# Mamba mixer stage: the residual moved from VectorE to ScalarE and GpSimd, and the next tile's squares moved into the loop over heads

## The reference, cut to what matters

```
residual = hidden_states
h = rmsnorm(hidden_states, norm_w)
z, xBC, dt = split(h @ in_proj.T)
xBC = silu(conv(xBC) + conv_b)          # causal convolution of width 4 over the tokens
dt = softplus(dt + dt_bias);  A = -exp(A_log)
y = scan over tokens: state = state * exp(dt*A) + dt*B*x;  y = state*C;  y += D*x
y = rmsnorm(y * silu(z), ssm_norm_w)
h = residual + y @ out_proj.T
```

## Time and profile before

| quantity | value |
|---|---|
| median of three runs | 2724.34 us (2722.08 to 2725.27) |
| the profiled execution | 2722.0 us, of which the span of instructions 2720.2 us |
| mixer, from the start to L912 of tile 7 | 830 us |
| one tile in the steady part (L912 to L912) | 101.11 to 101.13 us |
| granted TensorE clock, mean | 0.999 |

### The profile page before, as it was taken

The page is one execution under the profiler, slowest core; times in us unless marked ns, Lnnn a source line. Parts: engine busy times, 40 slices in busy tenths (PEclk is TensorE's granted clock), DMA queues, the critical chain, the costliest instruction groups (busy, mean ns, idle before and its releaser), DMA issues.

```text
span 2720.2 us, 42348 instructions
## 1 busy us (share of the span) xinstructions
PE 2659.7 (98%) x15264; PEld 2070.4 (76%) x15264; DVE 1523.4 (56%) x2561; ACT 1019.5 (37%) x2375; POOL 693.8 (26%) x594
## 2 busy tenths in 40 slices
PE   7999999999999999999999989999999999999999
PEld 5777777777778888888888867777777777777776
DVE  8787797797795322332233277777777774111122
ACT  6334334334434222122212255555555553222221
POOL 6553553553561101000100101322233322000000
PEclk9999999999999999999999999999999999999999
DMA  4001001101114101110111211110111124211111
GB/s 154 27 21 47 31 15 46 44 3 46 46 48 140 62 1 62 62 62 0 62 62 48 73 70 48 63 40 29 62 54 62 58 64 150 82 47 46 46 46 47
DMA packets 85482, 147.83 MB, mean 54 GB/s; under 512 B 4032, under 2 KB 17984, under 8 KB 85408
## 3 DMA queue, kind: packets, MB, share of 16 engines
q1 hardware_dynamic: 85408, 146.84, 15.7%
HBM read 113.27 MB, written 33.55 MB: 54 GB/s over the span
## 4 chain that ended last, share of the span: by engine, by line
PE 88%; DVE 8%; issue 2%; ACT 1%; DMA 1%; DVEq 0%; SPq 0%; POOL 0%; ACTq 0%; POOLq 0%
PE ps L75 22%; PE ps L77 22%; PE ps L76 22%; PE ps L1770 4%; PE ps L2133 4%; PE ps L816 2%; PE ps L1782 2%; PE ps L1761 2%; DVE mx_m L608 1%; DVE mx_cv L600 1%; PE ps L792 1%; PE ps L804 1%; PE ps L747 1%; PE ps L1714 1%; PE ps L844 1%
## 5 line engine op out<-in xcount | busy, mean ns | idle before, releaser
L1471 ACT ACTIVATE at_pr<-ps,at_nm 128x256 f32<-128x256 f32 x512 | 235.6, 473 | 201.7 <-DVE at_nm L1621 201.7
L1162 DVE TENSOR_TENSOR gm_m_lo<-gm_m,gm_m_hi 128x512 fp32r<-128x512 f32 (+1 forms) x88 | 61.1, 694 | 416.9 <-ACT gm_m_hi L1079 416.9
L75 PE MATMUL ps<-sh_u_hi,gm_gu_hi 128*128 128x512 f32 (+1 forms) x704 | 274.9, 390 | 0.0
L76 PE MATMUL ps<-sh_u_lo,gm_gu_hi 128*128 128x512 f32 (+1 forms) x704 | 274.8, 390 | 0.0
L77 PE MATMUL ps<-sh_u_hi,gm_gu_lo 128*128 128x512 f32 (+1 forms) x704 | 274.7, 390 | 0.0
L1627 DVE COPY at_pT<-ps 128x512 f32<-128x512 f32 x256 | 176.3, 689 | 138.5 <-PE ps L1770 136.4
L1073 ACT ACTIVATE gm_sg<-ps 128x512 f32<-128x512 f32 (+1 forms) x88 | 52.7, 599 | 517.6 <-PE ps L77 517.4
L543 POOL TENSOR_TENSOR mx_m<-mx_m,mx_g 128x512 f32<-128x512 f32 x128 | 185.4, 1448 | 86.3 <-DVE mx_m L610 86.1
L75 PE MATMUL ps<-sh_u_hi,qm_w_hi 128*128 128x512 f32 x512 | 201.6, 394 | 2.1 <-issue 1.1
L77 PE MATMUL ps<-sh_u_hi,qm_w_lo 128*128 128x512 f32 x512 | 199.6, 390 | 0.0
L76 PE MATMUL ps<-sh_u_lo,qm_w_hi 128*128 128x512 f32 x512 | 199.4, 389 | 0.0
(11 more groups left out here) (252 smaller groups left out, 6352.6 us busy)
## 6 DMA issues: line engine op xcount, KB each, us to landing
sh_xf<-x_scratch SPq DMA_DIRECT2D x16, 1024.0 KB, 7.5
mx_xr<-in_x SPq DMA_DIRECT2D x8, 1024.0 KB, 5.6
h_scratch<-mx_xr SPq DMA_DIRECT2D x8, 1024.0 KB, 5.1
sh_xf<-h_scratch SPq DMA_DIRECT2D x8, 1024.0 KB, 8.4
gm_xr<-in_x SPq DMA_DIRECT2D x8, 1024.0 KB, 7.3
gm_r<-h_scratch SPq DMA_DIRECT2D x8, 1024.0 KB, 6.1
x_scratch<-gm_r SPq DMA_DIRECT2D x8, 1024.0 KB, 5.2
at_cf<-in_ctxT SPq DMA_DIRECT2D x16, 512.0 KB, 3.9
```

Source lines behind the costliest of these rows:

```text
L75: nc.tensor.matmul(out, l_hi, r_hi, start=first, stop=False)
L76: nc.tensor.matmul(out, l_hi, r_lo, start=False, stop=False)
L1471: A(pr[h][:, t, :], SC[h][:, SEQ * t:SEQ * t + SEQ], ACT.Exp, bias=nm[:, 4 * n + h, t:t + 1], accum_out=sums[:, 2 * b + t, 4 * g + h:4 * g ...
```

## The change

- The residual of tiles 0 to 6 is no longer made by DVE. ACT copies a PSUM bank, scaled by `rg`, into m0 (`scale_out`), and GpSimd adds m0 to `xr`. The order of banks is 2, 3, 0, 1. The first two copies stand at the end of ACT's tile, the other two between its first and second tap of the next tile. Tile 7 keeps the old way.
- PE's wait before `conv_in(2)` for the whole residual becomes four waits, of `conv_in(2)` to `conv_in(5)`, each for the copy of its own bank. DVE's first scan of a tile waits for GpSimd's adds.
- The four squares of the next tile move from the convolution into the loop over heads, j = 0 to 3. The four norms move from j = 1 to 4 to j = 5 (two) and j = 6 (two).
- GpSimd makes the reciprocal roots for these norms after head 9 instead of before head 0.

```diff
+    OUT = (2, 3, 0, 1)
 # ACT
+        def scale_out(i, n):
+            t = OUT[n]
+            act.wait_ge(s["out"], KI * i + KI)
+            act.wait_ge(s["y"], KI * i + KI)
+            act.wait_ge(s["rg"], i + 1)
+            A(m0[t][:, :], ps[t][:, :], ACT.Copy, scale=rg[:, t:t + 1]).then_inc(s["ho"], 1)
...
             if step_0(i):
                 exp_ln(i)
+            else:
+                scale_out(i - 1, 2)
+                scale_out(i - 1, 3)
             tap(i, 1)
...
-                if n >= 5:
-                    square(i + 1, n - 5)
...
-                if 1 <= j <= TT:
-                    norm(i + 1, j - 1)
+                if j < TT:
+                    square(i + 1, j)
+                elif j in (5, 6):
+                    norm(i + 1, 2 * j - 10)
+                    norm(i + 1, 2 * j - 9)
...
                 exp_ln(i + 1)
+                scale_out(i, 0)
+                scale_out(i, 1)
 # POOL
-            first(i + 1)
...
+                if h == 9:
+                    first(i + 1)
             add_squares(i, 7)
-            at(pool, s["h1"], TT * i)
+            at(pool, s["ho"], TT * i)
...
+            for n, t in () if final(i) else enumerate(OUT):
+                pool.wait_ge(s["ho"], TT * i + n + 1)
+                G(xr[:, t, :], xr[:, t, :], m0[t][:, :], ALU.add).then_inc(s["h1"], 1)
 # DVE
+            if h == 0:
+                at(dve, s["h1"], TT * i)
...
-            for t in range(TT):
+            for t in range(TT) if final(i) else ():
                 V.scalar_tensor_tensor(xr[:, t, :], ps[t][:, :], rg[:, t:t + 1], xr[:, t, :], ALU.mult,
 # PE
+            if 2 <= n <= 5:
+                at(pe, s["ho"], TT * (i - 1) + n - 1)
             if n >= 4:
                 pe.wait_ge(s["cv"], 3 * NCONV * i + 3 * (n - 3))
-            elif n == 2:
-                at(pe, s["h1"], TT * i)
```

More of the change, by code:

```diff
@@ L345, in stage_mixer @@
     names = ("x0 xr st dtp dtc dtt in G dat bc zp xt y out ss a nab ee u ln c rec c2 sp dt dta da dah dal "
-             "dac tap cv sl Ge z xd sc M t g gs glo acc sse rg h1").split()
+             "dac tap cv sl Ge z xd sc M t g gs glo acc sse rg ho h1").split()
     s = {**sh.s, **{k: sem(f"mx_{k}") for k in names}}
     me.s = s
+    OUT = (2, 3, 0, 1)
     def ahead(i):
@@ L546, in main @@
                     add_squares(i, (h - 3) // 2)
+                if h == 9:
+                    first(i + 1)
             add_squares(i, 7)
-            at(pool, s["h1"], TT * i)
+            at(pool, s["ho"], TT * i)
             pool.wait_ge(s["sse"], i + 1)
             G(rg[:, :], v0[:, :], mhalf[:, :], ALU.pow).then_inc(s["rg"], 1)
+            if not final(i):
+                pool.wait_ge(s["xr"], 16 * i + 16)
+            for n, t in () if final(i) else enumerate(OUT):
+                pool.wait_ge(s["ho"], TT * i + n + 1)
+                G(xr[:, t, :], xr[:, t, :], m0[t][:, :], ALU.add).then_inc(s["h1"], 1)
         pool.wait_ge(su.dve, dve_0 + 4)
@@ L723, in main @@
                 dt_second(i + 1)
-            dve.wait_ge(s["out"], KI * i + KI)
-            dve.wait_ge(s["xr"], 16 * i + 16)
-            dve.wait_ge(s["rg"], i + 1)
-            for t in range(TT):
+            if final(i):
+                dve.wait_ge(s["out"], KI * i + KI)
+                dve.wait_ge(s["xr"], 16 * i + 16)
+                dve.wait_ge(s["rg"], i + 1)
+            for t in range(TT) if final(i) else ():
                 V.scalar_tensor_tensor(xr[:, t, :], ps[t][:, :], rg[:, t:t + 1], xr[:, t, :], ALU.mult,
```

## The result

| | before | after |
|---|---|---|
| median of six runs | 2724.35 us (2721.6 to 2725.27) | 2737.28 us (2736.12 to 2739.71) |
| ratio, 95% interval | | 1.005 [1.0037, 1.0063] |
| span of the profiled execution | 2720.2 us | 2734.8 us |
| one looped tile | 101.1 us | 103.0 us |

What follows compares the result with a forecast made beforehand. PE was taken to bound the kernel, with one 1.9 us hole a tile. 7 x 1.75 + 1.3 = 13.5 us slower gave 2735.5 against the profiled execution, 2737.8 as median; range 2731 to 2745, chance 0.80.

Steps and rivals of the forecast that it cites:

- The term that counts: Late norms behind ACT's square at j = 6 delay PE's next-tile transposes: 1.75 us in tiles 0 to 6, 1.3 in tile 7.
- The terms set at nothing: Moved residual, squares and root: each forecast to cost 0 and gain 0.
- The residual on ACT and GpSimd: Start of a tile: ACT's copies at 0.78 us and GpSimd's adds at 1.29 us fit without delaying PE; cost 0.
- The squares: Leaving the convolution shortens nothing, as ACT waited 1.11 us for PE before the tap; 0 on both sides.
- The root after head 9: GpSimd's two small instructions take about 1.3 us, head 11 keeps over 3 us of room before PE wants it; cost 0.
- the hole: PE's 1.9 us of waits per tile, for GpSimd's multiplied decays and ACT's silu; forecast to stay.
- (1): Rival: DVE's saved 2.73 us a tile close PE's 1.9 us hole, sum +0.2, 2724.5 us; chance 0.06.
- (2): Rival: the transposes' wait is hidden, PE coming later or the norms earlier, 2724.3 us; chance 0.05.
- (3): Rival: GpSimd's adds hold up DVE's small steps in `dt_third`, say 1 us a tile, +7, 2744.8 us; chance 0.04.
- (4): Rival: PE's new pause drops the granted clock, 1.45 us in each of seven tiles, 10.2, 2748.0 us; chance 0.03.

Runs made afterwards that it cites:

- experiment 1: Changed kernel with norms 0 and 1 at j = 4, norms 2 and 3 at j = 5: 2724.39 us, ratio 1.0004.
- experiment 2: Kernel before with only the norms moved, two at j = 5 and two at j = 6: 2738.15 us, ratio 1.0052.
- experiment 4: Changed kernel with three norms at j = 5 and one at j = 6: 2734.11 us, ratio 1.0036.
- experiment 3: Kernel before with only the residual moved to ACT and GpSimd; squares, norms and root as before: 2725.42 us, ratio 1.0006.
- experiment 6: Kernel of experiment 1 with the two first scans of a tile moved into the convolution: 2724.56 us, ratio 1.0005.
- experiment 7: Kernel before with the two first scans of a tile moved into the convolution: 2723.43 us, ratio 1.0001.
- experiment 8: Experiment 6 plus, in tiles 1 to 7, first x transposes, head 2's spread and scan ahead of the last convolution channel: 2714.5 us, ratio 0.9958.
- experiment 9: Experiment 7 plus, in tiles 1 to 7, first x transposes, head 2's spread and scan ahead of the last convolution channel: 2713.02 us, ratio 0.9954.
- experiment 5: Kernel of experiment 1 with DVE's wait for GpSimd's adds moved from before the first scan to before convolution channel 8: one execution, 2727.35 us.

## Why the prediction was right

**The term that counts.** The step was: the norm ends at 417.68, the transpose starts 1.75 us later than before, 7 times, and 1.3 more in tile 7. Measured: 1.72 a tile in tiles 1 to 6, from the same pieces (0.52, 1.32, 0.13 against 0.52, 1.33, 0.15), and tile 7 longer by 1.28 (100.05 against 98.77 from sum to sum), with the 0.35 that PE waited there before gone, as forecast. Experiments 1 and 2 show that this placement is necessary and sufficient for the loss, experiment 4 that the wait follows the length of ACT's queue.

**The terms set at nothing.** The residual on ACT and GpSimd: shown by experiment 3, and no wait of PE names them. The copies took 0.68 to 0.69 each, under the 0.78 taken. The squares: ACT's idle time in the convolution grew by what they had taken (the 1.11 us before the tap at 347.81 became 1.73). The root after head 9 cost GpSimd 1.7 us, 0.4 more than the 1.3 taken, and no wait of PE: head 11's second product was done at 405.32, and PE took it at 408.73, 3.4 us later.

**What was missed.** The change adds a wait to DVE's queue in front of the first scan, and I looked only at whether it would be satisfied. It stands on the chain that makes the hole, and its 0.09 us come 6 times, 0.5 us. It is too small for the runs and was found in the trace. A slip in the range, without effect: 7 times 1.60 and 1.3 are 12.5, not 12.3. Up to the end of the mixer the two profiled executions differ by 13.92 us: 1.54 in tile 0, 1.85 in each of six looped tiles, 1.28 in tile 7. That is the number to hold against the 13.5 of the sum. That the medians differ by 12.9, less than both, is partly chance: the profiled execution of the kernel before lay 2.3 us under its median, that of the changed kernel 0.7.

**The rivals.** (1) The hole closes: it stayed, for the reason given, the 1.78 us in front of channel 8. Experiments 6 to 9 add what the argument lacked: idle time of DVE there can be used, but only when PE's order hands over the work early enough. (2) left no trace. (3) came out as nothing, but was hardly put to the test: DVE's small steps ended as the adds began, and the next of them came at 341.76, 1.4 us behind the last add; only convolution instructions, which read PSUM, ran beside the adds. (4) Clock: at the pauses of 1.56 us the granted clock stayed at 1.00, 2.4 GHz. In the mixer it did fall once, to a mean of 0.69 over 4 us in tile 0 (1.2 GHz in part), at the end of a wait of PE of 3.20 us; the kernel before had 2.6 us of wait there and no fall. The length of that wait alone doesn't decide it: experiment 2 had 2.6 us and a fall, experiment 5 had 3.2 us and none. What a fall costs there is hidden, since DVE bounds tile 0 there: in experiment 1, with the mean at 0.50 in the same stretch, tile 0 ended at 124.4 as before.

**Left open.** Tile 0 ended between 124.4 and 128.1 us in the profiled executions of the nine experiments. Part of this is PE's pace at the start of the program. Here is the small projection of tile 0, first before, then in experiment 9:

```profile
15.62 1.07 PE L844 MATMUL ps<-sh_u_hi,mx_w_dt 128*32 128x512 f32 x8 [1.46 <-issue]
```

```profile
15.73 1.93 PE L851 MATMUL ps<-sh_u_hi,mx_w_dt 128*32 128x512 f32 x8 [1.46 <-issue]
```

In experiments 4, 5, 7, 8 and 9 it went at about half the pace, and the first channel's projection began at 19.2 to 19.3; in the two kernels and the other experiments it went as in the first row, and that projection began at 17.3 to 17.6. The edits don't sort the runs in this way. What remains, as the 2.3 us between experiments 8 and 9, is open. It is more than the differences between the medians of 6 and 7 or 8 and 9.

After the mixer, the profiled execution took 1890.3 us before, 1890.9 in the changed kernel and 1891.8 to 1892.8 in the nine experiments, whose edits don't touch that part. The granted clock goes with it: from 1580 to 1605 us its mean was 0.93 before and 0.86 in experiment 1; in the changed kernel it was lower in one more place, with a mean of 0.91 over 20 us from 2215, where before it was 1.00. So the tiles, and not the whole span of a single execution, carry the readings above.

## What to carry to other kernels

When an operation moves to a later place in an in-order queue, look at what is last in that queue before the bound engine's next wait, and add up the lengths from its last release: two operations of 0.7 us, harmless behind j = 5, cost 1.7 us a tile behind j = 6. Relief of an engine that is waited for only in one place counts only if it reaches that place; if the engine waits for the bound engine in between, it ends there. To close such a hole, move the bound engine's own small operations forward, so that the other has something to do in its idle time.

## What the runs showed of the hardware

- A semaphore wait that had long been satisfied cost DVE's queue about 0.09 us in the hardware loop (0.71 to 0.80 us from start to start, experiment 5), and nothing in tile 7, which is written out (0.66 in both kernels).
- A scaled copy of 128x512 from PSUM to SBUF on ACT took 0.69 us, and 0.57 to 0.59 from start to start in a row of two; the add of two SBUF tiles on GpSimd took 1.30 us beside DVE multiply-adds with one operand in PSUM (2.31 us for three, as without the adds), and neither slowed the other.
- The pauses of PE of 1.56 us, once in 103 us, left the granted clock at 1.00 (2.4 GHz) in the stretch of the tile. A pause of 2.6 to 3.2 us in tile 0 went with a fall in some executions and with none in others.
